# A two-layer cross-attention and feed-forward kernel: chunks turned by DMA, another order of the first stage, four rotating banks

## What is computed

```python
x = x + L0_xattn(layernorm(x), ctx)      # fake_quant(rows) @ fake_quant(ctx), 8-bit affine
x = x + L0_ffn(layernorm(x))             # mx_linear: fp6 rows, fp4 weights, blocks of 32
x = x + L1_xattn(layernorm(x), ctx, ctx) # 32 query heads, 8 key/value heads of 128, rope, mask, softmax
x = x + L1_ffn(layernorm(x))             # silu(x @ gate.T) * (x @ up.T) @ down.T

def _mx_linear(x, w):
    return jnp.matmul(_mx_quant(x, 3), _mx_quant(w, 1).T)
def _mx_quant(x, mbits):                 # per block of 32 along the contraction
    shared_exp = jnp.floor(jnp.log2(amax)) - 2
    scale = jnp.exp2(shared_exp)
    return _quant_elem(xb / scale, mbits) * scale
k = _apply_rope((key @ wk)...); v = value @ wv
```

## Time and profile before

| | |
|---|---|
| time, median of 3 runs | 702.54 us (702.11 to 702.93) |
| profiled execution | 702.53 us, its span 700.7 us |
| TensorE busy | 668.3 us (95%) |
| VectorE busy | 520.0 us (74%) |
| GpSimd busy | 463.3 us (66%) |
| ScalarE busy | 363.3 us (52%) |
| granted TensorE clock, mean | 1.000 |

### The profile page before, as it was taken

How to read it: one execution, slowest core, us unless ns; L and a number is a source line. 1 busy time by engine, 2 the same in 40 slices (tenths; PEclk the granted TensorE clock), 3 DMA queues, 4 the chain that set the end, 5 groups by cost and what they waited for, 6 DMA issues and landing times.

```text
span 700.7 us, 11095 instructions
## 1 busy us (share of the span) xinstructions
PE 668.3 (95%) x3152; PEld 494.0 (70%) x3152; DVE 520.0 (74%) x1046; ACT 363.3 (52%) x686; POOL 463.3 (66%) x407
## 2 busy tenths in 40 slices
PE   6999998899899999999999999999999999799997
PEld 2444443444577788888888888888888877688885
DVE  4999798777668888888888888888888886721122
ACT  2697434533565665666666665665665663211110
POOL 0697426432479878778789788688698478066661
PEclk9999999999999999999999999999999999999999
DMA  9985422140323132141131221221223012013311
GB/s 340 343 293 183 134 87 80 36 155 6 127 71 119 30 106 76 30 134 45 55 110 45 82 83 45 90 75 46 89 75 135 17 31 66 25 46 101 113 56 61
DMA packets 39420, 67.27 MB, mean 96 GB/s; under 512 B 3680, under 2 KB 12000, under 8 KB 38368
## 3 DMA queue, kind: packets, MB, share of 16 engines
q1 hardware_dynamic: 39392, 66.93, 28.9%
HBM read 57.48 MB, written 9.44 MB: 95 GB/s over the span
## 4 chain that ended last, share of the span: by engine, by line
PE 71%; POOL 10%; DVE 8%; issue 7%; ACT 2%; DMA 1%; SPq 0%; POOLq 0%; DVEq 0%; ACTq 0%
PE ps L663 16%; PE ps L665 16%; PE ps L664 16%; PE ps L731 11%; PE ps L696 7%; POOL mx_raw L1104 3%; POOL mx_w L1110 3%; PE ps L584 2%; PE ps L520 1%; DMA X<-in_x 1%; PE ps L536 1%; POOL prob L1161 1%; PE ps L620 1%; DVE mx_amax L1339 1%; DVE stats L1260 1%
## 5 line engine op out<-in xcount | busy, mean ns | idle before, releaser
L1009 ACT ACTIVATE prob<-ps,nmax 128x512 f32<-128x512 f32 x128 | 88.3, 690 | 97.4 <-DVE nmax L1487 97.0
L1161 POOL TENSOR_SCALAR prob<-prob,rinv 128x512 f32<-128x512 f32 x128 | 89.4, 698 | 73.7 <-DVE rinv L1494 73.6
L731 PE MATMUL ps<-xt,wq_sb 128*128 128x512 f32 x384 | 103.2, 393 | 3.8 <-DVE q_cos L1502 2.1
L1020 ACT CAST pT<-ps 128x512 fp32r<-128x512 f32 x128 | 75.1, 587 | 52.8 <-PE ps L696 51.9
L1487 DVE CUSTOM_DVE_ANT_0 ps<-ps,mask_sb 128x512 f32<-128x512 f32 x128 | 87.9, 687 | 6.7 <-PE ps L665 6.3
L1508 DVE TENSOR_TENSOR pT<-ps,pT 128x512 fp32r<-128x512 f32 x128 | 86.3, 674 | 3.0 <-ACT pT L1020 2.0
L731 PEld LDWEIGHTS ps<-xt,wq_sb 128*128 128x128 f32 x384 | 71.6, 188 | 22.0 <-issue 4.6
L696 PE MATMUL ps<-idf,prob 128*128 128x128 f32 x512 | 76.7, 272 | 0.4 <-POOL prob L1161 0.3
L696 PEld LDWEIGHTS ps<-idf,prob 128*128 128x128 f32 x512 | 63.8, 141 | 17.3 <-POOL prob L1161 1.6
L520 PE MATMUL ps<-ctxT,wk_sb 128*128 128x512 f32 x128 | 60.5, 613 | 6.5 <-DMA ctxT<-in_ctx_cols 6.5
L1104 POOL TENSOR_TENSOR mx_raw<-mx_raw,mx_r 128x2048 f32<-128x2048 f32 (+1 forms) x9 | 30.2, 3354 | 53.7 <-DVE mx_r L1347 53.7
(11 more groups left out here) (177 smaller groups left out, 1587.9 us busy)
## 6 DMA issues: line engine op xcount, KB each, us to landing
mx_raw<-in_mxw SPq DMA_DIRECT2D x8, 1024.0 KB, 5.5
wq_raw<-in_wq SPq DMA_DIRECT2D x32, 256.0 KB, 3.2
wo_raw<-in_wo SPq DMA_DIRECT2D x32, 256.0 KB, 2.7
v_scr<-v_st SPq DMA_DIRECT2D x16, 256.0 KB, 2.5
kr<-k_scr SPq DMA_DIRECT2D x16, 256.0 KB, 2.9
vr<-v_scr SPq DMA_DIRECT2D x16, 256.0 KB, 3.4
k_scr<-k_st SPq DMA_DIRECT2D x14, 256.0 KB, 2.1
kr_swp<-k_scr SPq DMA_DIRECT2D x28, 128.0 KB, 3.3
```

The source lines that it names most:

```text
L731: last = mm(query_bank(H), wq_sb[:, par, l, k], xt[:, r, k], start=(n == 0), stop=(n == 11))
L1009: nc.scalar.activation(prob[:, j], bank(j % 2), ACT.Exp, bias=nmax[:, j:j + 1], scale=-1.0, accum_out=rsum[:, j:j + 1]).then_inc(exps, 1)
L1020: copy(pT[:, v % 2, 0, :, i * P:(i + 1) * P], bank(2 + i % 2).rearrange("p (k c) -> p k c", k=4)).then_inc(ph_ready, 1)
L1161: nc.gpsimd.tensor_scalar(prob[:, i], prob[:, i], rinv[:, i:i + 1], 1.0, ALU.mult, ALU.mult).then_inc(probs, 1)
```

## The change

- **Loads.** x comes first, then the first context half and the first values half in four slices each (`slice_load(k)`, one 128-row slice of the contraction, 256 KB), with chunks 0 and 1 between them. wk, the second halves and the others follow.
- **First units.** TensorE begins with the four values units of step 0, slice by slice over four banks (`first_values`). Keys (0,0) are an ordinary unit of step 0, and keys (5,1) move from the late keys to step 7.
- **Banks.** `ROTATE` has four banks, (4, 5, 6, 7); the lifted halves lie in banks 0 and 2 and what follows.
- **Turns.** SP turns a chunk with one transposing transfer from `mx_w` to `WT` (`chunk_turn`), chunk i-1 in step i between the stores of its two parts, and the rows for the first attention with four (`rows_turn`, step 1). `mx_turn`, `mx_keep` and turn 0 of `turn_quantised` are gone. The rows for the network are still turned by TensorE. GpSimd's `scale_out(i)` waits for the turn of chunk i-2.
- **GpSimd.** `scale_in` and `scale_out` work in halves of 1024 columns, and ScalarE lifts a half when it is scaled; `mx_r` is made on GpSimd.
- **Second rows.** Layernorm and fp6 quantising both come in step 5, behind that step's clip and exponents; GpSimd's `fp6_out` too.
- **fp6.** The floor of the maximum and the factor 2^4 are one instruction: five instructions in `fp6` and one in `fp6_clip`, before six and two. The table `f6_e` has two buffers.
- **Head 0's keys** are stored unrotated and loaded with the swapped copy; GpSimd multiplies them behind tiles 1 and 2 of the network, VectorE adds them behind the third layernorm, and ScalarE's two casts wait for that.
- **Layernorm of one tile** uses two instructions a Newton step and one more at the end (seven), before three (nine).

```diff
-    ([("v", 0, 0), ("v", 1, 0), ("v", 2, 0), ("v", 3, 0)], [("k", 0, 1)]),
+    ([("v", 0, 0), ("v", 1, 0), ("v", 2, 0), ("v", 3, 0)], [("k", 0, 0), ("k", 0, 1)]),
...
-    ([("v", 7, 1), ("k", 5, 0)], []),
+    ([("v", 7, 1), ("k", 5, 0), ("k", 5, 1)], []),
-LATE_KEYS = ((5, 1), (6, 0), (6, 1), (7, 0), (7, 1))
-LATE_BANK = (3, 6, 2, 1, 3)
+LATE_KEYS = ((6, 0), (6, 1), (7, 0), (7, 1))
+LATE_BANK = (6, 2, 1, 3)
...
-ROTATE = (5, 6, 7)
-LIFT_BANK = (1, 3)
+ROTATE = (4, 5, 6, 7)
+LIFT_BANK = (0, 2)
...
+            def slice_load(k):
+                sp.dma_start(ctxT[:, k, 0:CTX], ctx_cols[k * P:(k + 1) * P, 0:CTX]).then_inc(ctxT0_in[k], 16)
+                sp.dma_start(wv_sb[:, k, 0:512], wv[k * P:(k + 1) * P, 0:512]).then_inc(wv0_in[k], 16)
...
+            def chunk_turn(i):
+
+                n = 1 if i == NFULL else MXT
+                sp.wait_ge(mx_ready, 2 * NFULL + 1 if i == NFULL else 2 * i + 2)
+                sp.dma_start(WT[:, MXT * i:MXT * i + n].rearrange("p t (k r) -> p (t k) r", r=P), mx_w[:, i % 2, 0:n * D],
+                             transpose=True).then_inc(WT_in[i], 16)
+
+            def rows_turn():
+                sp.wait_ge(q1_ready, NT)
+                for t in range(NT):
+                    sp.dma_start(q1T[:, :, t * P:(t + 1) * P], q1[:, t], transpose=True).then_inc(q1T_in, 16)
...
-                stores(STEPS[i][0] + STEPS[i][1])
+                stores(STEPS[i][0])
+                if i == Q_AT:
+                    rows_turn()
+                chunk_turn(i - 1)
+                stores(STEPS[i][1])
             k_load(6)
...
+            for i in range(NFULL - 1, NCH):
+                chunk_turn(i)
+            for i in range(NFULL - 1, NCH):
+                sp.wait_ge(WT_in[i], 16)
...
+            def first_values():
+
+                units = STEPS[0][0]
+                for k in range(KD):
+                    pe.wait_ge(ctxT0_in[k], 16)
+                    pe.wait_ge(wv0_in[k], 16)
+                    for unit in units:
+                        i = unit[1]
+                        last = mm(bank(rotating(unit)), ctxT[:, k, i * P:(i + 1) * P], wv_sb[:, k, 0:512], start=(k == 0), stop=(k == KD - 1))
+                        if k == KD - 1:
+                            last.then_inc(v_sums, 1)
...
             gate_up(0)
-            mx_turn(NFULL - 2, 0)
-            mx_turn(NFULL - 2, 1)
-            gate_up_slice(1, 0)
-            mx_turn(NFULL - 1, 0)
-            gate_up_slice(1, 1)
-            mx_turn(NFULL - 1, 1)
-            late_keys(0, range(0, 2))
-            gate_up_slice(1, 2)
-            mx_turn(NFULL, 0)
-            pe.wait_ge(mx_kept, 2 * NFULL + 1)
+            gate_up(1)
+            pe.wait_ge(mx_free, 2 * NFULL + 1)
             turn_inter(0)
             gate_up(2)
             down(0)
-            late_keys(0, range(2, 4))
             turn_inter(1)
...
             def scale_out(i):
                 pool.wait_ge(mx_rounded, i + 1)
-                after(pool, mx_turned, 2 * (i - 1))
-                n, p, e = width(i), i % 2, i % NRAW
-                tt(blocks(mx_w[:, p, 0:n]), blocks(mx_q[:, p, 0:n]), over(mx_e[:, e, 0:n // BLK], n // BLK), ALU.mult).then_inc(mx_ready, 1)
+                if i >= 2:
+                    pool.wait_ge(WT_in[i - 2], 16)
+                p, e = i % 2, i % NRAW
+                for cols in halves(i):
+                    n, lo = (cols.stop - cols.start) // BLK, cols.start // BLK
+                    tt(blocks(mx_w[:, p, cols]), blocks(mx_q[:, p, cols]), over(mx_e[:, e, lo:lo + n], n), ALU.mult).then_inc(mx_ready, 1)
...
+                if t in (1, 2):
+                    b = t - 1
+                    pool.wait_ge(kr_in[b], 48)
+                    tt(kr[:, b], kr[:, b], ropeK[:, 0], ALU.mult).then_inc(key_cosed, 1)
+                    tt(kr_swp[:, b], kr_swp[:, b], ropeK[:, 1], ALU.mult).then_inc(key_sined, 1)
...
                 chain(f6s, nc.vector.tensor_reduce(f6_amax[:, 0:m], blocks(src), AX.X, ALU.max, apply_absolute_value=True))
-                chain(f6s, ts(f6_amax[:, 0:m], f6_amax[:, 0:m], 2.0 ** -100, None, ALU.max))
                 chain(f6s, ts(f6_amax[:, 0:m].bitcast(U32), f6_amax[:, 0:m].bitcast(U32), EXP_MASK, None, ALU.bitwise_and))
-                chain(f6s, ts(f6_r[:, 0:m].bitcast(I32), f6_amax[:, 0:m].bitcast(I32), -1.0, float(0x7F000000), ALU.mult, ALU.add))
-                chain(f6s, ts(f6_r[:, 0:m], f6_r[:, 0:m], 2.0 ** -4, None, ALU.mult))
+                chain(f6s, ts(e, f6_amax[:, 0:m], 2.0 ** -100, 2.0 ** 4, ALU.max, ALU.mult))
+                chain(f6s, ts(f6_r[:, 0:m].bitcast(I32), e.bitcast(I32), -1.0, float(0x7F000000), ALU.mult, ALU.add))
...
+            for b in range(BATCH):
+                dve.wait_ge(key_cosed, b + 1)
+                dve.wait_ge(key_sined, b + 1)
+                tt(kr[:, b], kr[:, b], kr_swp[:, b], ALU.add).then_inc(key_roped, 1)
             rows_low()
```

314 lines of the change are left out of this document (124 added, 190 removed).

## The result

The changed kernel took **698.56 us** (median of 5 runs, 695.97 to 699.82) beside 702.93 us (702.11 to 705.67) for the kernel before on the same chip: a ratio of 0.9928, 95% interval 0.9907 to 0.9948. The forecast was 692.5, so the direction and the range (689.0 to 701.5) held, and the size was less than half: 4.4 us gained instead of 10. Its profiled execution is the slowest of the five, 699.82 us with a span of 698.0. Two more chips gave 698.47 and 698.30 us for the same kernel, and 700.96 and 700.73 for the kernel before, a ratio of 0.9964 [0.9950, 0.9978] and 0.9963 [0.9949, 0.9977]: there the gain is 2.5 and 2.4 us.

What follows compares the result with a forecast made beforehand. TensorE bounds the kernel except in the network, where VectorE sets the pace. First stage -8.0, network -3.1, head 0's keys +0.3 make -10.8; set back 0.8 to -10.0, from 702.53 to 692.5 us, range 689.0 to 701.5.

Steps and rivals of the forecast that it cites:

- The start: First loads: x down at about 5.7 us, TensorE's first product at 7.2, 0.75 us later than in the kernel before.
- TensorE's sum: First stage: counted TensorE work ends at 111.1 us, with turns and waits gone; the network starts 8.0 us sooner.
- From the turn to the network: TensorE from the last unit to the network's first product: 2.67 us as before, for a turn and two copies.
- The cover: End of first stage: quantised second rows ready at 103 us, 8 us ahead of TensorE's 111.1.
- The turns by DMA: SP's queue: T, the time of one 512 KB chunk turn, taken as 5 us; it decides from 10.4.
- The bound from packets: Chunk turns on SP's queue: upper bound of 10.5 us each, if every 256 B row were a packet.
- The slower rival: Turns on SP's queue cost 13 us or more per 512 KB, giving 710.7 us; chance 0.13.
- The network: Feed forward network: 3.1 us saved, from shorter quantising, a shorter wait in tile 1 and fewer small collisions.
- small collisions: Network: collisions with GpSimd's last chunk and late keys ahead of tile 3, worth some 0.5 us of gain.
- Head 0's keys at the end: Behind the last layernorm: two VectorE sums delay ScalarE by between 0 and 1.3 us, taken as 0.3.
- the set-back: Whole kernel: 0.8 us taken off the gain for waits no row shows, wv's margin and two ties.
- the first one, a smaller gain: Early transfers don't overlap, or network keeps its pace and first stage loses 3 us to SP's turns: 696.5 to 701.1; chance 0.18.

Runs made afterwards that it cites:

- e1_order: The changed kernel with ScalarE copying four of the last six units ahead of chunk 7's first lift, and its last lift behind q1T: 695.27 us, ratio 0.9925.
- e9_best: e5_late6 with GpSimd's `fp6_out` ahead of scaling chunk 8, and ScalarE's lift of chunk 8 behind q1T: 693.78 us, ratio 0.9903 to the kernel before.
- e5_late6: The changed kernel with the second rows' quantising back in step 6 and the layernorm ahead of step 5's clip: 695.99 us, ratio 0.9909 to the kernel before.
- e11_long_fp6: The changed kernel with the fp6 floor and the factor 2^-4 as instructions of their own again: 699.37 us, ratio 0.9979 to the kernel before.
- x1_after: The changed kernel unedited, run again on the third group's chip: 698.30 us, ratio 0.9963 to the kernel before.
- e3_filler: The changed kernel with 12 useless TensorE products between the second rows' turn and the network: 697.78 us, ratio 0.9950 to the kernel before.
- e7_fill_net: e1_order with 12 useless TensorE products ahead of the third slice of the network's tile 1: 695.52 us, ratio 0.9913 to the kernel before.

## Why the prediction was right in direction and wrong in size

The misfit against the profiled execution is 699.82 - 692.5 = 7.3 us (6.1 against the median). By the steps of the prediction:

**The start: nearly right.** 7.98 instead of 7.2. x was down at 6.25 instead of 5.7. The values took 16.4 us to 24.37; the forecast had 5.84 + 3 x 3.44 = 16.2. The second half of wv, with its one us of margin, was never waited for. +0.8.

**TensorE's sum: right, but not all of the path.** e1_order and e9_best have the turn at 111.6 and 111.8, and the sum gives 111.1 + 0.8. In the changed kernel the bank wait adds 1.36, and 0.3 are unaccounted. The step that failed is "a unit waits for a copy that had 10.3 us". That counts the banks' turn, and not what stands ahead of the copy in ScalarE's queue: lifts of chunk 7, which await VectorE. The prediction itself says that the step up "pushes back rounding chunk 6 and its turn", and looks only for who wants the turn. ScalarE's lifts want the rounding, and TensorE wants what is queued behind them. The banks then came free late by 1.36 us, and q1T by 1.7. e1_order, which alters nothing but that order, gives back 3.2 us.

**From the turn to the network: missed.** 4.40 us instead of 2.67, +1.7, by the same queue: the lift of chunk 8 ahead of q1T. Here too e1_order has 2.67.

**The cover: 2 us and not 8.** The rows came at 109.7 instead of 103. The layernorm started at 87.81 and not 86.0 (1.8) and took 11.6 us instead of 6.9 (4.7, nearly all of it the three held instructions); the rest is 0.2. The rows taken for it in the earlier trace rows were measured with GpSimd idle. The conclusion was worse than the number: "without the move a step up, this would be the next wait". e5_late6 leaves the quantising in step 6 and waits 0.29 us, with GpSimd's order put right (e9_best) nothing; the step up costs some 2.4 us. That it costs them through ScalarE's queue fits e1_order, whose 3.2 us come back with the step up in place.

**The turns by DMA: right.** T was taken as 5 us; the nine landed in 4.5 (2.8 to 8.4), and issuing one holds SP's queue for 2.2 us (1.6 to 6.3). TensorE never waited for a turned chunk. The bound from packets, 10.5, was far off: the page's packets rose by 19776 for eight and a quarter chunks and the rows with other loads among them, and their share only by 4.4 points. The slower rival, decided at 11.9, is out. The 1.4 us that the prediction estimated from the Trainium skill ("Advanced Engine Details and Errata", X-Bar Transpose (TRN2)) was too short as a time to landing: no turn landed in less than 2.5 us, not even one of 128 KB. These times contain the fixed part of a transfer, so no run here tests the rate itself. No run puts the turns back on TensorE alone either: what they are worth by themselves rests on the count, which came true as a whole.

**The network: 3.1 us forecast, 0.1 in the changed kernel, 1.1 in e9_best.** From its first product to the last down product it is 43.81 us before, 43.67 after (43.90 as the trace has it, without the missing record), 42.74 in e9_best, where the clock stays at 1.0 up to 690 us. By tiles (VectorE's clip to clip, the first from the network's start):

| | before | forecast | after | e9_best |
|---|---|---|---|---|
| tile 0 | 10.87 | -0.44 | 11.74 | 10.82 |
| tile 1 | 9.17 | -1.34 | 8.14 | 8.14 |
| tile 2 | 8.45 | -0.44 | 8.17 | 8.16 |
| tile 3 | 9.46 | -0.44 | 9.76 | 9.76 |
| last clip to last down product | 5.86 | | 5.86 | 5.86 |

Tiles 1 and 2 gained 1.03 and 0.28, which is 0.31 and 0.16 less than forecast: between the last product and the clip, the shorter form saves 0.31 us and not 0.44, and the third product of tile 1 still waits 1.50 us for its `silu`, where the forecast had it wait for VectorE's own work only. The prediction read the earlier trace rows as VectorE waiting "once inside a tile, else it works"; in tile 2 of the kernel before it waits 1.49 us too. In tile 0 the third slice's product came 5.49 us into the network before. In e9_best it comes at 6.25, as VectorE still rounds and clips the last chunks until 118.0, 3.6 us into the network. They were pushed back, and by this as well, beside GpSimd's scaling of the second rows (e9_best, VectorE):

```profile
107.51 3.61 DVE L1313 TENSOR_SCALAR mx_e<-mx_amax 128x16 uint32<-128x16 uint32 x1
```

The same instruction takes 0.17 us in the changed kernel, where GpSimd is idle. In the changed kernel VectorE is free after 118.9, 0.9 us in, but TensorE at the lower clock delivers the slice for a product at 7.17. e11_long_fp6, with VectorE as free and the clock at 1.00 there, has it at 5.49, so the low stretch costs the 1.7 us in full. Tile 3 pays for head 0's keys, where the forecast said that the rotation "lies in GpSimd's gaps". It does, but GpSimd's gaps are where VectorE works unheld (e9_best, VectorE):

```profile
148.28 0.19 DVE L1339 TENSOR_SCALAR f_e<-f_amax 128x44 f32<-128x44 f32 x1
148.51 1.14 DVE L1340 TENSOR_SCALAR f_r<-f_e 128x44 int32<-128x44 int32 x1
```

1.14 instead of 0.19 behind GpSimd's scaling of the first queries' weights, which the key rotation ahead of it had pushed to there. The changed kernel has the same 1.14 at 152.96. The 0.5 us set down for small collisions as a gain was a guess in the wrong direction.

**Head 0's keys at the end: nearly right.** From the last down product to the first query product it is 11.47 us before and 12.01 after, counted from 161.65, and 12.01 in x1_after and e9_best, whose records are whole: +0.5, where 0.3 was forecast out of 0 to 1.3.

**The rest of the kernel: missed.** Of 3.4 us at the first query product 2.7 are left at the end. The code from 200 us on is the same but for counts; at 600 to 605 us the clock is 0.66 where it was 1.00 before. The forecast had "from there on all as now". +0.7.

The sum: 0.8 + 1.7 + 1.7 + 3.0 + 0.2 + 0.7 - 0.8 (the set-back) = 7.3. Of it 3.1 us are the two waits in ScalarE's queue, which e1_order takes away. 1.7 in the network's first tile and 0.7 behind 600 us are clock, of which the forecast had no term; the network's other 1.3 are small VectorE instructions held by GpSimd, savings put too high and a gain that was guessed, less 0.4 won in its first tile.

How idle time and clock hang together is shown in part. In the changed kernel the gap of 3.34 us and the fall go together, and the 12 products that fill it take both away at that place, with six runs of twelve at 0.998 or more where 17 unfilled ones have none. It is not a rule: e9_best kept 1.00 behind a gap of 3.22, e5_late6's clock fell behind one of 1.57, and x1_after's behind one of 1.12 (low at 196 to 202 us) that the kernel before has as well. At 600 us both kernels have the same waits, 1.2 and 1.1 us, and only the changed one falls; why stays open.

Of the rivals the first one, a smaller gain, came true in its size, and its 698.6 beside 698.56 is luck. The network did keep its pace and the first stage did lose some 3 us, but in ScalarE's queue and not to SP's turns, and the pace was kept by gains and losses that cancel.

## What to carry to other kernels

When a step is moved up in one engine's order, list what it pushes back, then who waits for that, and then what is queued behind each waiter: here VectorE's rounding, ScalarE's lift, and behind the lift the copies that free TensorE's banks. A duration taken from a trace holds for its neighbours too; some small VectorE instructions took ten times as long beside a working GpSimd here (1.84 us and 0.17), and to move either only moves the bill, unless GpSimd idles. When a change opens an idle gap of TensorE, look at the granted clock behind it in several executions: it may cost the gap's time and up to 1.7 us more, and may not.

## What was not expected of the hardware

- **TensorE's clock** fell from 2.4 to 1.2 GHz behind a gap of 3.34 us (1.00 to 0.50 between 116 and 122 us), with 1.7 us lost, and runs of one kernel differ by 4 us with it (692.56 us at 1.0, 697.39 at 0.993). It also fell behind waits of 1.12 to 1.57, and stayed up behind one of 3.22. Twelve products of no use, in one gap each, kept it at 1.00 behind that gap in the profiled executions of e3_filler and e7_fill_net.
- **VectorE beside GpSimd**: instructions of four columns took 1.40 to 1.84 us instead of 0.17, ending with GpSimd's halves of 1.89, and one of 16 columns took 3.61 beside an instruction of 4.02.
- **DMA turns** of 512 KB landed in 4.5 us, of 128 KB in 2.8, with up to 6.3 us of SP's queue for one issue.
- **Slices of 256 KB** on a queue that is filled ahead started TensorE 4.1 us sooner than transfers of 1024 KB, at 404 GB/s from 10 to 20 us beside 408.
